# Three rounded products in place of one full-precision product in the q, k and v projections of a routed transformer layer

## The reference

```
x = layernorm(x + recurrence(x))                      # (2, 4096, 256)
weights = x @ router_w + router_b
topv, topi = top_k(weights, 512);  sel_idx = sort(topi[:, :511])
x_sel = x[sel_idx];  m_sel = mask[sel_idx][:, sel_idx]
hn = rmsnorm(x_sel, ln1)
q, k, v = rope(hn @ wq), rope(hn @ wk), hn @ wv       # 16 heads of 16
o = softmax(q k^T / 4 + m_sel) v @ wo
x1 = x_sel + o;  x2 = x1 + gelu(rmsnorm(x1, ln2) @ w1) @ w2
out = zeros.at[sel_idx].set(x2 * w_sel) + x * (1 - (weights > topv[:, -1:]))
x = layernorm(x + out)
```

## Time and profile before

| what | value |
|---|---|
| median of 3 runs | 508.66 us (506.38 to 574.14) |
| the profiled execution, time | 503.42 us |
| its span, first to last instruction | 501.7 us |
| PE busy in the span | 448.1 us (89%) |
| DVE busy | 400.8 us (80%) |
| ACT busy | 278.8 us (56%) |
| mean granted TensorE clock | 0.98 |

### The profile page before, as it was taken

How to read it: one execution, slowest core, us unless ns; L and a number is a source line. 1 busy time by engine, 2 the same in 40 slices (tenths; PEclk the granted TensorE clock), 3 DMA queues, 4 the chain that set the end, 5 groups by cost and what they waited for, 6 DMA issues and landing times.

```text
span 501.7 us, 10169 instructions
## 1 busy us (share of the span) xinstructions
PE 448.1 (89%) x3501; PEld 330.2 (66%) x3501; DVE 400.8 (80%) x1239; ACT 278.8 (56%) x586; POOL 172.7 (34%) x210
## 2 busy tenths in 40 slices
PE   7798999997999877998988999997998999998970
PEld 4687887786878632665765666665885666665860
DVE  7778988799788788869389999978768999967150
ACT  3536556544564542035659999944347999962200
POOL 9266677675776740363342000001000000000532
PEclk9999999998999999989999999999999999999995
DMA  7723423342232120168850000000000000000110
GB/s 246 230 43 103 151 86 96 117 124 84 85 98 72 45 83 1 32 204 266 269 155 2 2 2 1 3 2 0 1 1 1 3 2 1 3 3 0 37 38 11
DMA packets 29370, 33.89 MB, mean 68 GB/s; under 512 B 5860, under 2 KB 24968, under 8 KB 29320
## 3 DMA queue, kind: packets, MB, share of 16 engines
q1 hardware_dynamic: 23088, 24.78, 15.2%
q0 software_dynamic: 3520, 8.40, 5.7%
q10 hardware_dynamic: 2712, 0.06, 0.3%
HBM read 19.59 MB, written 13.63 MB: 66 GB/s over the span
## 4 chain that ended last, share of the span: by engine, by line
PE 48%; DVE 11%; POOL 9%; issue 7%; ACT 5%; POOLq 1%; DVEq 0%; ACTq 0%; another core or an unknown queue 0%
PE ps L979 11%; PE ps L994 7%; PE ps L963 6%; PE ps L1069 4%; POOL arena L509 3%; PE ps L1046 3%; PE ps L910 3%; PE ps L928 2%; POOL r L518 2%; PE ps L806 2%; PE ps L859 1%; PE ps L935 1%; PE ps L914 1%; ACT arena L1279 1%; PE ps L1052 1%
## 5 line engine op out<-in xcount | busy, mean ns | idle before, releaser
L1279 ACT ACTIVATE arena<-arena,nmax 128x511 f32<-128x511 f32 x128 | 91.5, 718 | 3.3 <-DVE nmax L1736 3.0
L1736 DVE CUSTOM_DVE_ANT_0 arena<-ps,nmask 128x511 f32<-128x511 f32 x128 | 84.8, 684 | 0.0
L979 PE MATMUL ps<-ident,arena 128*128 128x128 f32 x512 | 78.7, 276 | 3.5 <-ACT big L413 2.3
L979 PEld LDWEIGHTS ps<-ident,arena 128*128 128x128 f32 x512 | 58.7, 140 | 25.3 <-ACT arena L1279 15.0
L705 PE MATMUL ps<-wgd_hi,x_hi 128*128 128x512 f32 x128 | 51.6, 403 | 0.0
L963 PE MATMUL ps<-arena 96*128 96x512 bf16 x128 | 48.4, 384 | 2.5 <-DVE arena L1684 1.7
L707 PE MATMUL ps<-wgd_hi,x_lo 128*128 128x512 f32 x128 | 50.5, 394 | 0.0
L706 PE MATMUL ps<-wgd_lo,x_hi 128*128 128x512 f32 x128 | 50.4, 393 | 0.0
L413 DVE COPY big<-ps 128x512 f32<-128x512 f32 x64 | 44.1, 688 | 4.8 <-PE ps L979 3.6
L509 POOL TENSOR_TENSOR arena<-arena 128x512 f32<-128x512 f32 x32 | 41.2, 1289 | 11.7 <-DVE arena L1394 10.2
L413 ACT COPY big<-ps 128x512 f32<-128x512 f32 x64 | 36.9, 576 | 8.1 <-PE ps L994 6.6
(11 more groups left out here) (251 smaller groups left out, 1027.9 us busy)
## 6 DMA issues: line engine op xcount, KB each, us to landing
arena<-in_L_attn_x SPq DMA_DIRECT2D x16, 512.0 KB, 4.6
out<-ob_sb SPq DMA_DIRECT2D x16, 512.0 KB, 3.2
w_sb<-in_L_ffn_w SPq DMA_DIRECT2D x2, 1024.0 KB, 10.6
mt_scratch<-nmask SPq DMA_DIRECT2D x8, 256.0 KB, 4.4
mt_scratch<-big SPq DMA_DIRECT2D x8, 256.0 KB
big<-in_L_attn_Wg SPq DMA_DIRECT2D x1, 256.0 KB, 4.2
big<-in_L_attn_WD SPq DMA_DIRECT2D x1, 256.0 KB, 5.3
wqk<-in_L_ffn_wq SPq DMA_DIRECT2D x1, 256.0 KB, 7.6
```

Source lines behind the costliest of these rows:

```text
L979: mm = pe.transpose(ps[:, 2 + u % 2, k * P:(k + 1) * P], pr[u % 4][:, k * P:(k + 1) * P], ident[:, :])
L1279: act.activation(pr[u % 4][:, 0:K - 1], sm[u % 4][:, 0:K - 1], ACT.Exp, bias=nmax[:, c, h:h + 1], scale=-1.0, accum_out=rsum[:, c, h:h + 1 ...
L1736: dve.tensor_tensor_reduce(sm[u % 4][:, 0:K - 1], ps[:, S_BANKS[b][u % AHEAD], 0:K - 1], nmask[b][:, c, 0:K - 1], 1.0, 3.4e38, ALU.add, AL ...
```

## The change

The three products hi*hi, hi*lo and lo*hi take the place of the fp32 product in `project`, which is cut into `project_high` (the rounded high part of the tokens times both parts of the weights) and `project_rest` (the low part of the tokens times the high part of the weights). DVE forms the low part of the turned tokens (`rest_of_first`, eight subtractions of 256 columns from PSUM). ACT rounds the scaled weights to `wqk_hi` and `wv_hi`; PE forms weight minus high part in PSUM with an identity and a negated identity (`less`), in the place of 25 filling products of the search, and ACT copies the low parts out. The high part of w1 lies in the same memory as the new high parts, so its two copies (`high_of_w1`) move from the search into the first batch row's attention on ACT. The turned tokens use banks 2 and 3 for both batch rows, and the mask rows two banks in place of three. `copy_mask` moves from DVE to ACT, and DVE's order around `rope`, `parts` and `odd_mask_rows` changes.

```
+            def less(o, w, hi):
+                pe.matmul(o, ident[:, :], w, start=True, stop=False)
+                return pe.matmul(o, minus_ident[:, :], hi.bitcast(F32), start=False, stop=True)
+            def rest_of_qk(k):
+                pe.wait_ge(gain_ready, 2 * KD + 1)
+                less(ps[:, 3 + k, :], wqk[:, k, :], wqk_hi[:, k, :]).then_inc(w_lo_done, 1)
+            def rest_of_v():
+                for k in range(KD):
+                    mm = less(ps[:, 5 + k, 0:D], wv_sb[:, k, :], wv_hi[:, k, :])
+                mm.then_inc(w_lo_done, 1)
...
             count(1, 5)
-            fill(7, 13)
+            rest_of_qk(0)
+            rest_of_v()
             count(1, 6)
-            fill(7, 12)
+            rest_of_qk(1)
             pick_rows(0)
...
-                    elif tile >= 3:
-                        pe.wait_ge(*turned_ready((tile - 3) // (MS // P), (tile - 3) % (MS // P)))
+                    elif tile >= 2:
+                        pe.wait_ge(*turned_ready((tile - 2) // (MS // P), (tile - 2) % (MS // P)))
...
+            def project_high(b, c):
+                pe.wait_ge(w_lo_ready, KD + 1)
+                pe.wait_ge(hnT1_ready[b], c + 1)
...
+                for o, hi, lo in outputs(c):
+                    for k in range(KD):
+                        for w in (hi, lo):
+                            pe.matmul(o, hnT_hi[:, k, c * P:(c + 1) * P], w[:, k, :],
+                                      start=(k == 0 and w is hi), stop=False)
+            def project_rest(b, c):
+                pe.wait_ge(hnT1_lo_ready, b * C + c + 1)
+                for (o, hi, _), signal in zip(outputs(c), (qk_done, v_done)):
+                    for k in range(KD):
+                        mm = pe.matmul(o, first_lo[:, k, c * P:(c + 1) * P], hi[:, k, :], start=False, stop=(k == KD - 1))
+                    mm.then_inc(signal[b], 1)
...
-            project(0, range(1))
+            project_high(0, 0)
+            pick_all(1)
+            project_rest(0, 0)
             turn_first_hn(0, 2)
-            pick_all(1)
             project(0, range(1, 2))
...
+            def high_of_w1(k):
+                act.wait_ge(w_ready, KD)
+                act.wait_ge(v_done[1], C)
                 act.copy(w1_hi[:, k, :], w1_sb[:, k, :]).then_inc(w_ready, 1)
...
+                        if b == 0 and u == 3 and hg in (1, 2):
+                            high_of_w1(hg - 1)
...
             copy_turned(0, 2)
+            copy_mask()
             copy_turned(0, 3)
...
+            def rest_of_first(b, c):
+                dve.wait_ge(hnT1_ready[b], c + 1)
+                at = slice(c * P, (c + 1) * P)
+                dve.tensor_tensor(first_lo[:, :, at], ps[:, X_BANK[c % 2], 0:D].rearrange("p (k n) -> p k n", k=KD),
+                                  hnT_hi[:, :, at].bitcast(F32), ALU.subtract).then_inc(hnT1_lo_ready, 1)
...
             one_hots(1)
+            rest_of_first(0, 0)
+            rest_of_first(0, 1)
             factors(0)
             angles(0)
             cosines(0)
             rows(1)
-            for c in range(C):
-                rope(0, c)
-                if c == 1:
-                    factors(1)
-                    angles(1)
-                    parts(0, 0)
+            rope(0, 0)
+            rest_of_first(0, 2)
+            rest_of_first(0, 3)
+            rope(0, 1)
+            parts(0, 0)
+            rest_of_first(1, 0)
+            factors(1)
+            angles(1)
+            rest_of_first(1, 1)
+            rope(0, 2)
+            rest_of_first(1, 2)
+            rope(0, 3)
+            rest_of_first(1, 3)
+            odd_mask_rows()
             parts(0, 1)
-            odd_mask_rows()
             for c in range(C):
                 copy_turned(0, c)
                 if c < 2:
                     parts(0, 2 + c)
-                elif c == 2:
-                    copy_mask()
```

More of the change, by code:

```diff
@@ L300, in build @@
         hnT1_ready = sems("hnT1_ready")
+        hnT1_lo_ready = sem("hnT1_lo_ready")
+        w_lo_done = sem("w_lo_done")
+        w_lo_ready = sem("w_lo_ready")
         hnT_done = sem("hnT_done")
@@ L882, in turn_first_hn @@
                 pe.wait_ge(x_sel_in[b][c], 16)
[L883 to L886 removed]
+                if b * C + c >= 2:
+                    pe.wait_ge(hnT1_lo_ready, b * C + c - 1)
                 for k in range(KD):
[L888 removed]
+                    mm = pe.transpose(ps[:, X_BANK[c % 2], k * P:(k + 1) * P], x_sel[b][:, c, k * P:(k + 1) * P], ident[:, :])
                 mm.then_inc(hnT1_done[b], 1)
@@ L899, in project @@
+            def project_rest(b, c):
[4 more added lines that the diff above has]
+                    mm.then_inc(signal[b], 1)
             def project(b, chunks):
-                pe.wait_ge(w_ready, KD)
                 for c in chunks:
-                    pe.wait_ge(hnT1_ready[b], c + 1)
-                    if c >= 2:
-                        pe.wait_ge(qk_ready[b], c - 1)
-                        pe.wait_ge(v_ready[b], c - 1)
-                    elif b > 0:
-                        pe.wait_ge(qk_ready[b - 1], c + C - 1)
-                        pe.wait_ge(v_ready[b - 1], c + C - 1)
-                    for k in range(KD):
-                        mm = pe.matmul(ps[:, 4 + c % 2, :], hnT[:, k, c * P:(c + 1) * P], wqk[:, k, :],
-                                       start=(k == 0), stop=(k == KD - 1))
-                    mm.then_inc(qk_done[b], 1)
-                    for k in range(KD):
-                        mm = pe.matmul(ps[:, 6 + c % 2, 0:D], hnT[:, k, c * P:(c + 1) * P], wv_sb[:, k, :],
-                                       start=(k == 0), stop=(k == KD - 1))
-                    mm.then_inc(v_done[b], 1)
@@ L918, in _ @@
+                    project_high(b, c)
+                    project_rest(b, c)
             psb = ps[:, :, :].bitcast(BF16)
@@ L1211, in _, with low_of_qk @@
             act.wait_ge(w2_loaded, 16 * (7 + 2 * HG))
-            act.mul(q_gain[:, :], ln_col[:, 0, :], -(HD ** -0.5)).then_inc(gain_ready, 1)
+            act.mul(q_gain[:, :], ln_col[:, 0, :], -(HD ** -0.5))
+            act.mul(minus_ident[:, :], ident[:, :], -1.0).then_inc(gain_ready, 1)
             act.wait_ge(gain_ready, 1)
             for k in range(KD):
-                g1, g2 = ln_col[:, 0, k:k + 1], ln_col[:, 1, k:k + 1]
+                g1 = ln_col[:, 0, k:k + 1]
                 act.mul(wqk[:, k, 0:D], wqk[:, k, 0:D], q_gain[:, k:k + 1])
                 act.mul(wqk[:, k, D:2 * D], wqk[:, k, D:2 * D], g1)
-                act.mul(wv_sb[:, k, :], wv_sb[:, k, :], g1)
-                act.mul(w1_sb[:, k, :], w1_sb[:, k, :], g2).then_inc(w_ready, 1)
+                act.mul(wv_sb[:, k, :], wv_sb[:, k, :], g1).then_inc(gain_ready, 1)
             for k in range(KD):
-                act.wait_ge(w_ready, k + 1)
+                act.wait_ge(gain_ready, k + 2)
+                act.copy(wqk_hi[:, k, :], wqk[:, k, :])
+                act.copy(wv_hi[:, k, :], wv_sb[:, k, :]).then_inc(gain_ready, 1)
+            for k in range(KD):
+                act.mul(w1_sb[:, k, :], w1_sb[:, k, :], ln_col[:, 1, k:k + 1]).then_inc(w_ready, 1)
+            def low_of_qk(n, k):
+                act.wait_ge(w_lo_done, n)
+                act.copy(wqk_lo[:, k, :], ps[:, 3 + k, :]).then_inc(w_lo_ready, 1)
+            low_of_qk(1, 0)
+            act.wait_ge(w_lo_done, 2)
+            act.copy(wv_lo[:, :, :], ps[:, 5:5 + KD, 0:D]).then_inc(w_lo_ready, 1)
+            low_of_qk(3, 1)
+            def high_of_w1(k):
+                act.wait_ge(w_ready, KD)
+                act.wait_ge(v_done[1], C)
                 act.copy(w1_hi[:, k, :], w1_sb[:, k, :]).then_inc(w_ready, 1)
@@ L1228, in copy_first_hnT @@
                     act.wait_ge(v_done[b - 1], c + 1)
-                act.copy(hnT[:, :, c * P:(c + 1) * P], ps[:, X_BANK[b][c % 2], 0:D].rearrange("p (k n) -> p k n", k=KD)
+                act.copy(hnT_hi[:, :, c * P:(c + 1) * P], ps[:, X_BANK[c % 2], 0:D].rearrange("p (k n) -> p k n", k=KD)
                          ).then_inc(hnT1_ready[b], 1)
@@ L1255, in value, with copy_mask @@
                 act.mul(v_sb[b][:, c, :], ps[:, 6 + c % 2, 0:D], wf_sel[:, b, c, 2:3]).then_inc(v_ready[b], 1)
+            def copy_mask():
+                for c in range(C):
+                    act.wait_ge(nm_done[0], c + 1)
+                    act.copy(nmask[0][:, c, :], ps[:, M_BANKS[c], :]).then_inc(nm_ready[0], 1)
             def copy_turned(b, c):
```

35 lines of the change are left out of this document (20 added, 15 removed).

## The result

| | before | after |
|---|---|---|
| median of the runs | 507.52 us (4 runs, 504.34 to 574.14) | 514.28 us (4 runs, 512.59 to 516.59) |
| the profiled execution, time | 503.42 us | 512.59 us |
| its span | 501.7 us | 510.8 us |
| mean granted clock of the profiled run | 0.98 | 0.957 |

A forecast was written before the change was run, and what follows sets the result against it. PE held 48% of the chain, but hand-overs between engines were taken to end the edited stage. 503.42 - 1.0 (earlier exponentials) + 0.8 (w1's copies) = 503.2, or 506.0 us on the scale of the 506.2 mean; range 500.0 to 511.5.

The forecast's parts named there:

- the search: Before the pick: PE's low parts, 3.44 us, fit the fillers' place of 3.64 us; cost 0.
- the price of the products: In the projections: rounded products cost 0.23 us at 512 columns and 0.115 at 256, a chunk 2.07 us.
- the pick: PE's pick waits for angles delayed by DVE's two first subtractions, starting 0.7 us later, at 217.1.
- the pair of tiles on two banks: Second batch row's mask tiles: 1.3 us a pair through PE, drain and DVE's copy; 6.5 us for eight.
- DVE's chain from the odd copies to the last split: Before the exponentials: three parts and three pairs of copies, 12.4 us, ending at 258.6; mask copies (2.64 us) moved to ACT.
- The rival of weight loads: In the projections: 0.19 us loads pace the 256-column products, PE's saving falls to about 0.6 us; 507.5 us, chance 0.10.
- the price of ACT's late starts in the first mask stretch: First to second row's mask tiles: ends at 239.4 without late starts, 240.8 with both; 239.8 taken.
- the margin of some 4 us: POOL's gathers for batch row 1 come 0.7 us later; their data still land in time, cost 0.
- From the split to the exponential: First split to first exponential: 17.5 us, before 18.53; exponentials start at 263.8 against 264.78, a gain of 1.0 us.
- w1's copies: In attention on ACT: at most 0.71 us each reaches PE, 0.4 taken, 0.8 for both; bounds 0 and 1.98.
- The clock: Rival: idle PE before the pick prolongs the lower clock, projections lose 1.7 us more; 509.2 us, chance 0.18.
- PE's 4.1 us: In the projections: rounded chunks save PE 0.51 us each, 4.1 us over eight, the most this part can give.

The follow-up runs named there:

- e11_changed_cols: Changed kernel with POOL's four issues of the second batch row's mask columns moved behind its first turn of attention; ratio to the kernel before 1.0107.
- the last experiment: e9_cols plus ten fillers ahead of the fourth mask tile and six behind the first four scores; ratio to the kernel before 0.9991.
- e4_w1: Kernel before with only the two copies of w1's high part moved from the search into the first batch row's attention; ratio 1.0013.
- e3_nofill: Kernel before with only the 25 fillers ahead of pick_rows left out; ratio 1.0027.
- e8_all: Changed kernel with 12 fillers, first subtractions behind the angles, three mask-row banks, and w1's copies back in the search; ratio to the kernel before 0.9999.
- e9_cols: e8_all plus POOL's issues of the second batch row's mask columns moved behind its first turn of attention; ratio to the kernel before 1.001.
- four repairs and more: The kernels e8_all, e9_cols and the last experiment; ratios to the kernel before 0.9999, 1.001 and 0.9991.

## Why the prediction was wrong

**Right**: the search (200.69), the price of the products (a chunk 2.12 us, forecast 2.07), the pick (217.30, forecast 217.1), the pair of tiles on two banks (1.43 us by DVE's copies, forecast 1.3; 6.64 for the eight, forecast 6.5), DVE's chain from the odd copies to the last split (251.1 to 263.5: 12.4, forecast 12.4). The rival of weight loads falls: the 256-column products follow each other at 0.12 us, though each load is recorded at 0.19. The Trainium skill's statement that FP32 gets no fast weight load ("TensorE: Matmul & The Clock Gate", section "Weight-path perf modes") decides nothing here.

**The step that failed** is the price of ACT's late starts in the first mask stretch: "Whether ACT's late starts come back the trace can't say, since nothing in it explains them: without them the stretch ends at 229.2 + 10.2 = 239.4, with both at 240.8. I take 239.8." It ended at 244.67, 14.7 us behind its start in place of 10.6: 4.1 of the 9.4 us by which the profiled execution (512.59) lies above the sum of 503.2. The mechanism was named, but bounded at 1.4 us without a working, although ACT had idled 2.2 us in the rows and PE, by the prediction's own count, 2.6.

The part without late starts was right: with plain transfers the stretch takes 10.33 us (231.08 to 241.41), forecast 10.2. So the late starts cost 4.3 us. PE's stand ahead of the third tile makes 3.0 of them (3.51 us, there 0.52), and the work behind it, in part at the lower clock, 1.3. They were hardly longer than before (2.8 us, 2.2 before), but met more. The pick came 0.9 us later, the issues ended 1.5 us later, ACT stood still until 1.3 us behind them, with four products of PE in front of it in place of two, and with two banks PE stood still too (with three it did so one tile later). Even where ACT idled only 0.86 and 0.87 us, in the kernel with the subtractions behind the angles, the stretch takes 13.5 us. I had moved the gathers past the pick and asked only when their data land ("I cost that at 0: the margin of some 4 us covers it"); the margin held, the issuing collided. Shown by the runs with the gathers held back, with plain transfers and with small gathers. One pair of profiles doesn't mislead here: the kernel with the mask columns later (e11_changed_cols) has the same code up to the first split and takes 20.60 us from the first mask rows to there, the changed kernel 21.30.

**From the split to the exponential** I forecast a gain of 1.0 us; it lost 0.1. DVE's chain did shrink, but the second set of POOL's issues now ended at 264.85, behind the start of the last split. With the issues moved away the stretch takes 16.9 us: the gain was there, and more than forecast. An estimate from the two runs without late starts, which no run has together: 217.30 + 12.71 + 16.97 + 16.90 = 263.9 for the first exponential, forecast 263.8.

**w1's copies** cost 0.7 each, the value of my first bound and not the 0.4 that I took. The mechanism was right; the lead of PE's that was to take up another 0.28 us of each copy doesn't show.

**The clock** was the rival to which I gave 0.18, at the wrong place. Between the pick and the mask rows are 0.6 us more than forecast (12.71, forecast 12.1), with the clock at 0.50 to about 224 in place of 222.5; that the clock alone makes them isn't shown. The falls that I didn't see stand behind PE's later waits. The exponentials lose 1.1 us between the first and the 13th, and the fillers of the last experiment bring that to 0.1. They lose 1.4 us between the 64th and the 65th, in the feed-forward block. With w1's 1.4 these are the 3.9 us of the last row of the table. The loss at the 65th comes and goes, so it can't be put down to the change: in the single profiles the kernel before with w1's copies alone (e4_w1) loses 1.05 us there and the one with more fillers 1.25, while e3_nofill, e8_all, e9_cols and e11_changed_cols lose nothing. The Trainium skill, "TensorE: Matmul & The Clock Gate", section "Part 1: The HAM clock gate", speaks of a default that is throttled until activity releases it; the fillers of the last experiment agree (0.52 to 1.00). Why the clock also falls inside a pick in which PE issues without a break no run here shows.

**Where PE's 4.1 us went.** PE has been given them (2.12 us a chunk), but the stage's end is set by hand-overs to ACT and DVE beside POOL's issues. With four repairs and more the ratio is 0.9991 to 1.001: the saved work doesn't reach the end there. Late starts at the mask rows are left in all three profiles, and a full kernel without them was not run.

What stays open: by what path POOL's issuing holds up other engines, and how the 6.8 us of the medians divide; the table divides one pair of profiled executions, each of which is the fastest of its kernel.

## What to carry to other kernels

When a change moves a gather that POOL issues, ask what the other engines hand over while it issues, not only when its data land; a wait in the trace that nothing explains is to be given its price at the new place, not its old size. Work taken off PE turns into idle time where another engine hands over, and that can cost the clock: fill it, or leave the work. Fewer banks are cheap as long as the engine that empties them is on time: here 1.3 us on eight tiles (6.64, with three banks 5.33). A third bank doesn't cover an engine that is 4 us late.

## What the runs showed of the hardware

While POOL issues indirect gathers (most of them 0.93 to 1.25 us each), ACT and DVE start late on products that PE has finished, ACT up to 4.2 us (the fillers given back) and DVE 1.7 us (the changed kernel, 264.2 to 265.89). In the fourteen profiles that have these issues beside the first mask tiles, ACT's last late start lies 0.7 to 1.7 us behind the last issue of mask rows (1.63 before the change, 1.27 after it); behind the last issue of mask columns it is 0.9 to 1.0 in the changed kernel. Plain transfers at 95% of the DMA engines' time don't do it. The Trainium skill, "SBUF — State Buffer", section "SBUF: two separate sides", lets only DVE and GpSimd wait for each other at a port, and ACT for nobody; ACT's late starts of up to 4.2 us are not told by it; by what path they come no run here shows.

The time of one and the same kernel goes with its mean clock: of 31 runs of the kernel before, the four at 0.963 to 0.966 took 509.4 to 509.7 us, the two at 0.979 and 0.980 took 504.8 and 503.9, some 3.3 us for each 0.01 over all 31. Which of the two brings the other these figures don't tell. The changed kernel's four runs lie at 0.954 to 0.957. A single profiled run at 0.98, as the one read for the prediction, shows the kernel at its best.
